# Scores ahead of transposes, row maximum ahead of remainder, exponential ahead of rounding in a causal attention kernel

## What is computed

```python
q = (x @ Wq + bq).reshape(b, h, t, dh)
k = (x @ Wk + bk).reshape(b, t, h, dh).transpose(0, 2, 3, 1)
v = (x @ Wv + bv).reshape(b, t, h, dh).transpose(0, 2, 1, 3)
logits = jnp.einsum('bhtd,bhds->bhts', q, k) * scale
weights = jax.nn.softmax(logits + mask, axis=-1)
out = jnp.einsum('bhts,bhsd->bhtd', weights, v)
return out.transpose(0, 2, 1, 3).reshape(b, t, h * dh) @ Wo + bo
```

## Time and profile before

| | |
|---|---|
| median of 3 runs | 1260.04 us (1259.06 to 1260.85) |
| profiled execution, its own time | 1261.86 us |
| its span, first to last instruction | 1260.1 us |
| busy, PE / PEld | 1233.5 us (98%) / 1116.5 us (89%) |
| busy, DVE / ACT / POOL | 879.8 (70%) / 738.2 (59%) / 737.1 us (58%) |
| mean granted TensorE clock | 0.997 |

### The profile page before, as it was taken

One profiled execution on the slowest core, in us unless ns is written; L12 is line 12 of the kernel. 1 busy time (PEld: TensorE's weight loads), 2 busy tenths in 40 slices (PEclk: granted clock), 3 DMA queues, 4 the chain that ended last, 5 costly groups with the idle time before them and its releaser, 6 DMA issues.

```text
span 1260.1 us, 22029 instructions
## 1 busy us (share of the span) xinstructions
PE 1233.5 (98%) x8286; PEld 1116.5 (89%) x8286; DVE 879.8 (70%) x1694; ACT 738.2 (59%) x1533; POOL 737.1 (58%) x772
## 2 busy tenths in 40 slices
PE   8999999999999999999999999999999999999997
PEld 6788888888899999889999998899999889999996
DVE  7877777776576667666677676677667666677665
ACT  4544444444466666656666674666666656666663
POOL 6355455454476775527666672576775527666663
PEclk9999999999999999999999999999999999999999
DMA  6100000000000000110000002010000100000001
GB/s 156 38 9 13 14 13 7 26 2 17 5 22 14 14 26 5 47 42 14 18 22 5 22 14 72 14 55 14 14 26 6 46 26 14 18 22 7 12 6 34
DMA packets 57337, 29.96 MB, mean 24 GB/s; under 512 B 16272, under 2 KB 57232, under 8 KB 57232
## 3 DMA queue, kind: packets, MB, share of 16 engines
q1 hardware_dynamic: 56016, 27.62, 7.9%
q10 hardware_dynamic: 1216, 0.93, 0.2%
HBM read 26.44 MB, written 2.10 MB: 23 GB/s over the span
## 4 chain that ended last, share of the span: by engine, by line
PE 89%; DVE 5%; ACT 4%; issue 1%; DMA 1%; POOL 0%; SPq 0%; ACTq 0%; DVEq 0%
PE ps L41 27%; PE ps L43 26%; PE ps L42 26%; PE ps L1067 8%; DVE k_lo L734 2%; ACT k_hi L394 2%; PE ps L942 1%; ACT q_all L345 1%; DMA acc<-in_x 1%; DVE pt_lo L781 0%; DVE probs L877 0%; DVE xn_rows L683 0%; DVE sgn L706 0%; PE ps L1033 0%; DVE acc L746 0%
## 5 line engine op out<-in xcount | busy, mean ns | idle before, releaser
L645 POOL TENSOR_TENSOR inv_sum<-row_sum,minus_one 128x1 f32<-128x1 f32 x256 | 140.9, 550 | 309.5 <-ACT probs L430 307.7
L648 POOL TENSOR_TENSOR probs<-probs,inv_sum 128x128 f32<-128x128 f32 (+7 forms) x256 | 296.3, 1158 | 20.1
L781 DVE TENSOR_TENSOR pt_lo<-ps,pt_hi 128x512 fp32r<-128x512 f32 (+3 forms) x384 | 204.0, 552 | 97.5 <-ACT pt_hi L416 97.3
L430 ACT ACTIVATE probs<-probs,neg_max 128x128 f32<-128x128 f32 (+7 forms) x256 | 198.0, 774 | 61.2 <-DVE neg_max L877 58.5
L416 ACT ACTIVATE pt_hi<-ps 128x512 fp32r<-128x512 f32 (+3 forms) x384 | 174.2, 489 | 85.6 <-PE ps L1067 85.6
L877 DVE CUSTOM_DVE_ANT_0 probs<-ps,mask_row 128x128 f32<-128x128 f32 (+7 forms) x256 | 192.0, 750 | 2.7
L42 PE MATMUL ps<-pt_lo,v_hi 128*128 128x256 f32 (+1 forms) x640 | 180.1, 281 | 0.0
L43 PE MATMUL ps<-pt_hi,v_lo 128*128 128x256 f32 (+1 forms) x640 | 180.0, 281 | 0.0
L1067 PE MATMUL ps<-ident,probs 128*128 128x128 f32 x1152 | 172.4, 277 | 2.6 <-DVE pt_lo L781 1.9
L41 PE MATMUL ps<-pt_hi,v_hi 128*128 128x256 f32 (+1 forms) x640 | 173.2, 271 | 1.6 <-DVE pt_lo L781 1.6
L628 POOL TENSOR_TENSOR hid_lo<-act_buf,hid_hi 128x512 fp32r<-128x512 f32 x64 | 82.7, 1292 | 145.1 <-ACT hid_hi L369 145.1
(11 more groups left out here) (111 smaller groups left out, 3209.7 us busy)
## 6 DMA issues: line engine op xcount, KB each, us to landing
wq_in<-in_wq SPq DMA_DIRECT2D x63, 128.0 KB, 2.4
kv_in<-in_wk SPq DMA_DIRECT2D x16, 256.0 KB, 2.8
wo_in<-in_wo SPq DMA_DIRECT2D x32, 128.0 KB, 2.0
kv_in<-in_wv SPq DMA_DIRECT2D x32, 128.0 KB, 2.3
out<-acc SPq DMA_DIRECT2D x8, 256.0 KB, 2.6
acc<-in_x SPq DMA_DIRECT2D x2, 512.0 KB, 5.6
raw<-in_gate SPq DMA_DIRECT2D x16, 64.0 KB, 1.8
raw<-in_up SPq DMA_DIRECT2D x16, 64.0 KB, 2.0
```

The costliest lines, as they stand in the source:

```text
L430: nc.scalar.activation(probs[:, s % 4, 0:width], probs[:, s % 4, 0:width], ACT.Exp, bias=neg_max[:, s % 16:s % 16 + 1], scale=-1.0, accum_ ...
L645: nc.gpsimd.tensor_tensor(inv_sum[:, at], row_sum[:, at], minus_one[:], ALU.pow).then_inc(inv_done, 1)
L648: nc.gpsimd.tensor_tensor(row, row, inv_sum[:, at].to_broadcast([P, (i + 1) * P]), ALU.mult).then_inc(probs_done, 1)
L781: nc.vector.tensor_tensor(pt_lo[where], T[at % 2][:, 0:blocks * P].rearrange("p (a b) -> p a b", b=P), pt_hi[where].bitcast(F32), ALU.subt ...
```

## The change

Nothing is added or removed. On three engines the work inside a step is put in another order.

```diff
@@ scalar engine, for s in range(NH * TILES)
                 evacuate(job_of(h, LATE_AT.get(i - 1)))
-                if s >= LAG:
-                    pt_high(s - LAG)
                 evacuate(job_of(h, FIRST_AT.get(i)))
                 if i > 0 and not eager(h, i - 1) or i == 0 and h > 0:
                     exps(s - 1)
+                if s >= LAG:
+                    pt_high(s - LAG)
                 evacuate(job_of(h, EARLY_AT.get(i)))
@@ vector engine
-                between = FIRST_AT.get(i) == "O0a"
                 if i - 1 in LATE_AT:
                     evacuate(job_of(h, LATE_AT[i - 1]))
-                if s >= LAG:
-                    pt_low(s - LAG, 0)
-                    if between:
-                        evacuate(job_of(h, FIRST_AT[i]))
-                    if banks_of((s - LAG) % TILES) > 1:
-                        pt_low(s - LAG, 1)
-                if not between or s < LAG:
-                    evacuate(job_of(h, FIRST_AT.get(i)))
-                hurry = EARLY_AT.get(i) == "O1a"
-                if hurry:
-                    evacuate(job_of(h, EARLY_AT[i]))
+                evacuate(job_of(h, FIRST_AT.get(i)))
                 dve.wait_ge(scores_done, s + 1)
...
-                if not hurry:
-                    evacuate(job_of(h, EARLY_AT.get(i)))
+                if s >= LAG:
+                    for ch in range(banks_of((s - LAG) % TILES)):
+                        pt_low(s - LAG, ch)
+                evacuate(job_of(h, EARLY_AT.get(i)))
@@ tensor engine
                 h, i = divmod(s, TILES)
+                run(job_of(h, FIRST_AT.get(i)))
+                scores(s)
                 if s >= LAG:
                     transposes(s - LAG)
-                run(job_of(h, FIRST_AT.get(i)))
-                scores(s)
                 run(job_of(h, EARLY_AT.get(i)))
```

## The result

The changed kernel takes 1378.51 us (median of 4 runs, 1377.27 to 1380.68) against 1259.55 us before (median of 4). The ratio is 1.0943, with a 95% interval of 1.0930 to 1.0957: 9.4% slower. Forecast were 1346 us and a range up to 1376, so the direction is right and the time lies just above the range. 119 us were lost where 86 were expected.

What follows compares the result with a forecast made beforehand. TensorE was taken to bound the kernel. Waits at T6' (56.4 + 0.6), T0 (12.6) and O1b (24.6), less K1's 8.1, made 86.1 us on 1260.0: about 1346 us, range 1315 to 1376.

Steps and rivals of the forecast that it cites:

- What bounds the kernel, and direction: Plain heads: TensorE, busy 49.88 of 50 us, sets the time; an order gains only by closing its gaps; slower overall, 0.95.
- T6' for the first chunk of T5': Steps 0 and 1: T6' waits 1.88 us for its bank in heads 1 to 30; head 31 pays 0.59 more.
- T0 for the first chunk of T7': Steps 2 and 3: T0 waits 0.45 us for the bank of T7's first chunk, in 28 heads, 12.6 us.
- O1b for O1a's addition: Steps 4 to 6: O1b waits 0.88 us for bank M, freed by DVE's addition, in 28 heads, 24.6 us.
- K1's wait: K1's wait for `k_lo`, 0.27 us a head, goes; 30 heads give 8.1 us back.
- Covered waits: Everything else, such as K0 behind Vb, O0a behind K1 and Vb behind O1b, stays covered and costs nothing.
- the feeding of the query projections: Heads 7, 15 and 23: it changes by less than 1 us a head, put at nothing.
- The sum of the waits: All heads: 86.1 us in all, 2.94 us longer for a plain head.
- the clock falls: Rival, chance 0.04: the clock falls after each T6' wait, T6' and K1 take twice their time, 63 us more, 1409 us.
- only the long wait is real: Rival, chance 0.07: the two shorter waits, T0's and O1b's, close; 48.9 us remain, 1309 us.
- it gets faster: Rival, chance 0.03: T5's chunk leaves its bank before S1 ends, leaving only K1's gap to gain, 1252 us.
- nothing happens: Rival, chance 0.02: engines drift so far apart that orders inside a step do not matter, 1260 us.

Runs made afterwards that it cites:

- e3_fill: The changed kernel with 24 unread products of 128 columns put between S1 and T6', where TensorE otherwise waits: 1352.18 us, ratio 1.0730.
- e2_hurry: The changed kernel with DVE adding O1a ahead of tile 5's maximum again: 1370.59 us, ratio 1.0874.
- e5_act_dve_alone: The kernel before with ACT's and DVE's part of the change alone, TensorE in its old order: 1514.69 us, ratio 1.2035.
- e1_round_first: The changed kernel with ACT rounding a chunk of transposes ahead of the exponential again, still behind K0's rounding: 1332.07 us, ratio 1.0561.
- e4_pe_alone: The kernel before with TensorE's part of the change alone, ACT and DVE in their old order: 1468.14 us, ratio 1.1656.

## Why the prediction was right and where it was wrong

**What bounds the kernel, and direction.** Right. TensorE had 0.27 us a head to win and the new order uncovered three waits.

**T6' for the first chunk of T5'.** Forecast 1.88 us in heads 1 to 30. It lengthens the head by 2.06 (head 17). Every link of the chain had its forecast size but the last: TensorE resumes 0.14 us after DVE when it is a transpose that waits, and the 0.05 had been taken from a projection (rows 3, 5). The other half of the difference is the cover: S0 takes 883.54 - 883.26 = 0.28 us here, and the 0.36 of rows 3 had been used.

**T0 for the first chunk of T7'.** Forecast 0.45, measured 0.54 in 28 heads; the same link.

**O1b for O1a's addition.** Forecast 0.88, measured 0.89, and 0.10 more in its first slot. Its weights come late too: in the same 29 places the weight loads wait 25.3 us for `acc`, the products 21.2.

**K1's wait.** Gone as forecast. With its late first slot it had cost 0.33 rather than 0.27 us.

**Covered waits.** All that the prediction priced at nothing stayed closed. The one term put at nothing that was not is the feeding of the query projections: they gained 1.5 us in each of three heads.

**The sum of the waits** was 86.1 us, or 2.94 us for a plain head. At full clock a plain head takes 29.65 us instead of 26.35, 3.3 more. The sum over all heads at full clock is 1352.2 - 1260.5 = 91.7 us (e3_fill). The measured terms say the same: 30 x (2.06 - 0.33) + 28 x 0.54 + 28 x 0.99 + 0.5 for head 31 - 4.5 = 90.7. This part was 5.6 us short. The errors that the prediction names for it (0.2, 0.2 and 0.4 us) come to 22.8 us when all have one sign, not to the 28 that it states; 5.6 is well inside either. Some of that closeness is luck: without the 4.5 us of the query projections, which it did not forecast, it would have been some 9 to 10 us short.

**The clock is the step that failed.** Of the 32.5 us between 1346 and 1378.5, 26.3 are the clock's (e3_fill). The prediction took 1.00 for granted and gave the rival "the clock falls" 0.04, although it had noted that 1.88 us was longer than any wait of attention that its rows show at full clock. What the row with the wait of 1.29 us shows (rows 9, 10) ends at 1.29. The rival's place was right, behind T6', and its price was too high: 2.1 us in 30 heads, 63 in all, where 1.57 us in 17 heads, 27 in all, were measured. As a possible addition to every case, and not as a case of its own in place of the forecast, it would have moved the upper end of the range to where the time lay. By the Trainium skill (TensorE: Matmul & The Clock Gate, section "Why this matters for your kernels"), idle gaps between bursts of matmuls bring the clock down, but the gaps that it warns of are longer than these. Here the clock fell behind single gaps of 1.9 us in 17 heads, and the measurement decides.

**Rivals.** That only the long wait is real, that it gets faster, and that nothing happens are refuted by the waits list and the times.

**Which heads, and what is left open.** The work around the wait is the same in all plain heads, yet the clock fell in 17 heads and not in 13. In three of the 13 (heads 8, 16 and 24) the idle time is 1.73 us. For the other ten the trace shows a difference in time. All moments at which the granted clock changes in it lie whole multiples of one step apart, whatever the heads do: the stretches of heads 19, 20, 21 and 23 begin at 946.8, 977.5, 1008.3 and 1069.7 us, 30.7 us or twice that apart, while the heads last 29.65 or 31.2. Continue this series through the heads in which the clock did not change: in the 17 heads the first such moment after the wait began came at its end (at most 0.07 us before it) or up to 0.97 us behind; in the ten it came 0.11 to 1.25 us before the end, inside the wait. In e2_hurry 24 of the 27 waits of this length go by the same rule; in the other three the wait began less than 0.1 us behind such a moment, and the clock stayed. In e5_act_dve_alone even five waits of 2.9 us, with such a moment near their middle, left it at 1.00. So the number of heads that lose time depends on how the heads fall against these moments, and it changed from 17 to 20 when the heads got 0.6 us shorter. This is read off the traces; no run moved a wait on purpose, and what the chip measures between two such moments stays open.

## What to carry to other kernels

Where three engines follow hand-written orders, price a move by the bank or buffer that must come free: from the producer's end along every engine's queue, what stands ahead of the evacuation there, against the work that is left as cover on the bound engine. Do it for all engines together, since half of a consistent reordering can be far worse than the whole. And once a forecast opens a wait on TensorE that is longer than any its trace shows at full clock, the clock belongs in the sum as a term with its own bounds: from nothing to every such wait, since waits of one length can be punished in some places and not in others.

## What was not expected of the hardware

- The granted clock of TensorE fell to the 1.2 GHz level behind single waits of 1.9 us with dense work on both sides, and cost 1.57 us each time. Behind waits of 1.3 us and less, in the kernel before and in e1_round_first, it stayed at 2.4 GHz in attention. Three single waits of 1.73 us in each of the changed kernel and e2_hurry (heads 8, 16 and 24) left it there too. But length alone does not decide: ten of the changed kernel's waits of 1.9 us and five of 2.9 us in e5_act_dve_alone left it at 1.00, and in e4_pe_alone it fell once behind two waits of 0.87 and 0.78 us close together.
- 24 small unread products in the wait (1.51 us in all) kept it there, and made a kernel with more work 26 us faster.
- A gain of 0.6 us a head was half lost because the number of slow stretches went from 17 to 20: time saved on one wait can change what the clock does behind another.
- The granted clock changes only at moments that lie whole multiples of one step apart in a trace, and a wait of 1.9 us in the changed kernel brought it down where the next moment of this series came at the wait's end or later (17 of 17 heads), and not where it came at least 0.1 us before the end (10 of 10).
- After DVE's release a waiting transpose starts 0.14 us later, a waiting projection 0.05, with 0.10 more in the projection's first slot.
